# A feature-crossing ranking model on one core: eight fields of the second tile made by products, and a shorter pause ahead of each gather

## What is computed

```python
e = stack([tbl_f[ids[:, f]] for f in range(24)], axis=1)      # 1024 x 24 x 16
def cin(X0, Ws):                                              # three layers of 64
    Xk = X0
    for W in Ws:
        Xk = einsum('bfd,bhd,fho->bod', X0, Xk, W.reshape(24, Xk.shape[1], 64))
        outs.append(Xk.sum(axis=2))
    return concatenate(outs, axis=1)
h = concatenate([cin(e, (W0, W1, W2)), dense_ctx], axis=1)
y = relu(relu(h @ W_top1 + b_top1) @ W_top2 + b_top2) @ W_top3
```

## Time and profile before

| | |
|---|---|
| median of 3 runs | 396.9 us (392.81 to 399.77) |
| the profiled execution: its time | 396.69 us |
| the profiled execution: its span | 394.8 us |
| mean granted TensorE clock | 0.978 of full speed |
| busy: PE, DVE, ACT, POOL | 356.2, 305.0, 185.2, 245.0 us |
| busy share: PE, DVE, ACT, POOL | 90%, 77%, 47%, 62% |
| moved by DMA | 71.07 MB, mean 180 GB/s |

### The profile page before, as it was taken

The page is one execution under the profiler, slowest core; times in us unless marked ns, Lnnn a source line. Parts: engine busy times, 40 slices in busy tenths (PEclk is TensorE's granted clock), DMA queues, the critical chain, the costliest instruction groups (busy, mean ns, idle before and its releaser), DMA issues.

```text
span 394.8 us, 6950 instructions
## 1 busy us (share of the span) xinstructions
PE 356.2 (90%) x2624; PEld 156.3 (40%) x2624; DVE 305.0 (77%) x299; ACT 185.2 (47%) x347; POOL 245.0 (62%) x348
## 2 busy tenths in 40 slices
PE   0866899999919999999999996999999999999997
PEld 0545422423302334444433342434352445343475
DVE  2881399699618899989889967979798979998700
ACT  1120024352032457584647428565656486646464
POOL 5888888888888888888878888888880000000000
PEclk9999899999967999999999999899999999999999
DMA  7557958970999879994999789998998899750000
GB/s 208 166 115 154 235 116 175 229 167 6 202 239 253 204 157 235 255 262 94 225 249 237 146 201 261 248 203 200 250 250 202 186 247 247 210 161 0 2 2 2
DMA packets 56885, 71.07 MB, mean 180 GB/s; under 512 B 31154, under 2 KB 36018, under 8 KB 56851
## 3 DMA queue, kind: packets, MB, share of 16 engines
q1 hardware_dynamic: 49138, 69.04, 73.4%
q0 software_dynamic: 5632, 1.45, 3.6%
q10 hardware_dynamic: 2080, 0.13, 0.4%
HBM read 50.15 MB, written 1.58 MB: 131 GB/s over the span
## 4 chain that ended last, share of the span: by engine, by line
PE 46%; DMA 21%; issue 12%; DVE 11%; SPq 5%; ACT 2%; POOL 2%; ACTq 0%; DVEq 0%; POOLq 0%
PE ps_x L405 28%; DMA B_sb<-x_sb 9%; DVE Z L382 7%; PE ps_tower L405 7%; PE ps_b L405 6%; DMA C<-x_scratch 4%; PE ps_turn L405 4%; DMA A<-x_scratch 3%; DVE Z L345 2%; PE ps_turn L458 2%; SPq L257 2%; DMA small_ids_sb<-small_ids 1%; DMA x_scratch<-x_rows 1%; POOL x_rows L215 1%; DMA x_rows<-tbl,ids_sb 1%
## 5 line engine op out<-in xcount | busy, mean ns | idle before, releaser
L382 DVE TENSOR_TENSOR Z<-A,ps_b 128x1024 f32<-128x1024 f32 x192 | 221.0, 1215 | 8.4 <-PE ps_x L405 4.1
L215 POOL DMA_INDIRECT x_rows<-tbl,ids_sb x176 | 184.6, 1049 | 51.9 <-POOL pause_sb L226 31.7
L405 PE MATMUL ps_x<-Z,w_sb 128*64 128x512 f32 x768 | 185.2, 601 | 0.7 <-DVE Z L382 0.5
L372 DVE TENSOR_TENSOR Z<-A,C 128x1024 f32<-128x1024 f32 x48 | 58.2, 1225 | 49.4 <-DMA A<-x_scratch 24.5
L405 PEld LDWEIGHTS ps_x<-Z,w_sb 128*64 128x64 f32 x768 | 49.4, 137 | 81.0 <-issue 61.3
L405 PE MATMUL ps_x<-Z,w0s_sb 128*64 128x512 f32 x192 | 48.3, 625 | 16.6 <-DVE Z L372 15.0
L226 POOL MEMSET pause_sb<- 128x288 f32 x168 | 60.2, 358 | 0.2
L690 ACT ACTIVATE x_diag<-ps_turn,mask_sb 128x192 f32<-128x192 f32 x128 | 50.6, 606 | 11.9 <-PE ps_turn L466 7.8
L673 ACT COPY ps_b<-B_sb 128x1024 f32<-128x1024 f32 x36 | 36.9, 1026 | 14.2 <-DMA B_sb<-x_sb 13.8
L703 ACT COPY G<-ps_turn 128x416 f32<-128x416 f32 x31 | 15.7, 506 | 52.5 <-PE ps_turn L405 46.9
L405 PEld LDWEIGHTS ps_turn<-x_diag,x_rows 128*64 128x64 f32 x496 | 25.1, 137 | 17.8 <-issue 16.1
(11 more groups left out here) (60 smaller groups left out, 182.7 us busy)
## 6 DMA issues: line engine op xcount, KB each, us to landing
A<-x_scratch SPq DMA_DIRECT2D x48, 512.0 KB
B_sb<-x_sb SPq DMA_DIRECT2D x72, 256.0 KB
C<-x_scratch SPq DMA_DIRECT2D x32, 512.0 KB
x_rows<-tbl,ids_sb POOLq DMA_INDIRECT x176
x_quarters<-x_scratch SPq DMA_DIRECT2D x16, 96.0 KB
x_scratch<-x_rows SPq DMA_DIRECT2D x7, 192.0 KB
small_ids_sb<-small_ids SPq DMA_DIRECT2D x2, 512.0 KB, 5.3
w_sb<-w SPq DMA_DIRECT2D x2, 384.0 KB
```

Of the source, the lines that this page charges most:

```text
L215: pool.indirect_dma_start(out=x0_rows[t % 2][:, f * D:(f + 1) * D], out_offset=None, in_=tables[f], in_offset=bass.IndirectOffsetOnAxis(ap ...
L372: nc.vector.tensor_tensor(Z[s % ZR][:, :], A[u % AS][i][:, :], C[u % 2][i][:, :], ALU.mult).then_inc(z_ready, 1)
L382: nc.vector.tensor_tensor(Z[s % ZR][:, :], A[u % AS][i][:, :], ps_b[j % 2][:, :], ALU.mult)\
L405: return nc.tensor.matmul(out, lhsT, rhs, start=start, stop=stop)
```

## The change

Fields 8 to 15 (set 0) of tile 1 are no longer gathered but made by products with ones, as they are for tile 0. `MADE` lists what is made so, as pairs of tile and set. GpSimd gathers 16 fields of tile 1 and not 24, and its pause writes 144 columns and not 288.

The ids of the third set are read into `small_ids_sb[0]` once the cast of set 0 of tile 0 has read it: SyncE waits for that ahead of this load, and so ahead of the loads of the identity and the first weights. VectorE makes the new ones behind the preparation of the weights and ahead of the first `cross1`. TensorE multiplies them in the same loop, so `turn_small(1)` now stands behind the third chunk of the new set, and `turn_small(2)` behind its last. ScalarE copies the result into `x0_rows[1]`, and `store_tile(1)` waits for it too.

```diff
-PAUSE = 288
+PAUSE = 144
+MADE = ((0, 0), (0, 1), (1, 0))
...
-    HOT = [(k, c) for k in range(SETS) for c in range(chunks[k])]
+    HOT = [(m, c) for m, (t, k) in enumerate(MADE) for c in range(chunks[k])]
...
+        def gathered_fields(t):
+            made = [k for m, k in MADE if m == t]
+            return [f for f in range(F) if f < FR or f // FR - 1 not in made]
+        def gathers(t):
+            return sum(len(gathered_fields(m)) for m in range(1, t + 1))
...
-                for f in range(F):
+                for n, f in enumerate(gathered_fields(t)):
                     pool.memset(pause_sb[:, :], 0.0).then_inc(paused, 1)
-                    pool.wait_ge(paused, F * (t - 1) + f + 1)
+                    pool.wait_ge(paused, gathers(t - 1) + n + 1)
...
+            sp.wait_ge(small_ids_ready, SETS + 1)
+            src = small_ids[SETS:SETS + 1, :].to_broadcast([CR, FR * TILE_ROWS])
+            sp.dma_start(small_ids_sb[0][:, :], src).then_inc(next_ids_in, 16)
             sp.dma_start(id_sb[:, :], ident).then_inc(ident_in, 16)
...
             def store_tile(t):
-                sp.wait_ge(gathered[t % 2], 16 * F * ((t + 1) // 2))
+                if t % 2 == 1:
+                    sp.wait_ge(gathered[1], 16 * (gathers(1) + F * (t // 2)))
+                else:
+                    sp.wait_ge(gathered[0], 16 * F * (t // 2))
+                if t == 1:
+                    sp.wait_ge(small_ready, len(MADE))
...
+            make_ones(0)
+            make_ones(1)
             dve.wait_ge(mask_in, 16)
...
+            make_ones(2)
             for i in range(NI):
                 cross1(0, i)
...
-                if c == 2 and k > 0:
-                    turn_small(0)
-            turn_small(SETS - 1)
+                if c == 2 and m > 0:
+                    turn_small(m - 1)
+            turn_small(len(MADE) - 1)
             keep_warm(WARM[0])
...
-            for k in range(SETS):
-                act.wait_ge(hot_used, sum(chunks[:k + 1]))
+            for m, (t, k) in enumerate(MADE):
+                act.wait_ge(hot_used, made_hot[m])
...
-                act.wait_ge(small_ready, k + 1)
-                store_rows(act, 0, slice(FR * (k + 1), FR * (k + 2)), part_stored[k + 1])
+                if t == 0:
+                    act.wait_ge(small_ready, m + 1)
+                    store_rows(act, 0, slice(FR * (k + 1), FR * (k + 2)), part_stored[k + 1])
```

More of the change, by code:

```diff
@@ L71, in cin_tower @@
     CR = small_tables.shape[0]
-    HOT = [(k, c) for k in range(SETS) for c in range(chunks[k])]
+    SETS_AT = [sum(chunks[:k]) for k in range(SETS)]
+    HOT = [(m, c) for m, (t, k) in enumerate(MADE) for c in range(chunks[k])]
+    made_hot = [sum(chunks[k] for t, k in MADE[:m + 1]) for m in range(len(MADE))]
     x0_dram = nc.dram_tensor("x0_scratch", [TILES, F, 2 * COLS], F32, kind="Internal").ap()
@@ L218, in gather @@
                 ).then_inc(landed, 16)
-            for f in range(FR):
+            for f in gathered_fields(0):
                 gather(0, f, first_gathered)
@@ L338, in _, with make_ones @@
             dve.wait_ge(small_rows_in, 16)
-            for n, (k, c) in enumerate(HOT):
-                if c == 0:
+            def make_ones(m):
+                t, k = MADE[m]
+                if t == 0:
                     dve.wait_ge(small_ids_in[k], 16)
-                    nc.vector.tensor_copy(small_ids_f32[k][:, :], small_ids_sb[k][:, :]).then_inc(small_ids_ready, 1)
-                    dve.wait_ge(small_ids_ready, SETS + k + 1)
-                after(dve, hot_used, n - ZR + 1)
-                nc.vector.tensor_scalar(Z[n % ZR][0:CR, :], small_ids_f32[k][:, :], small_rows_sb[:, c:c + 1],
-                                        None, ALU.is_equal).then_inc(hot_ready, 1)
+                else:
+                    dve.wait_ge(next_ids_in, 16)
+                nc.vector.tensor_copy(small_ids_f32[k][:, :], small_ids_sb[k][:, :]).then_inc(small_ids_ready, 1)
+                dve.wait_ge(small_ids_ready, SETS + m + 1)
+                for c in range(chunks[k]):
+                    n = HOT.index((m, c))
+                    after(dve, hot_used, n - ZR + 1)
+                    nc.vector.tensor_scalar(Z[n % ZR][0:CR, :], small_ids_f32[k][:, :], small_rows_sb[:, c:c + 1],
+                                            None, ALU.is_equal).then_inc(hot_ready, 1)
+            make_ones(0)
+            make_ones(1)
             dve.wait_ge(mask_in, 16)
@@ L906 @@
         "ids": ids.reshape(TILES, 128, F).transpose(1, 0, 2).reshape(128, TILES * F),
-        "small_ids": ids[0:TILE_ROWS, FR:].transpose(1, 0).reshape(SETS, FR * TILE_ROWS),
+        "small_ids": np.concatenate([ids[TILE_ROWS * t:TILE_ROWS * (t + 1), FR * (k + 1):FR * (k + 2)].transpose(1, 0)
+                                     .reshape(1, FR * TILE_ROWS) for t, k in MADE]),
         "small_tables": small_tables.reshape(FR, sum(chunks), cr, D).transpose(2, 1, 0, 3),
```

25 lines of the change are left out of this document (18 added, 7 removed).

## The result

| | before | after |
|---|---|---|
| median of 4 runs each | 395.21 us (392.81 to 399.77) | 377.41 us (375.55 to 380.43) |
| ratio, with its 95% interval | | 0.9576 (0.9471 to 0.9682) |
| the profiled execution: time, span | 396.69, 394.8 us | 375.55, 373.7 us |
| mean granted TensorE clock | 0.978 | 0.991 |

Faster, by 17.8 us between the medians and by 21.1 us between the two profiled executions, where 12.4 were forecast. The profiled execution of after was the fastest of its four, so what follows splits a gain that is somewhat larger than the usual one. Two later measurements of the same kernel gave 376.17 us, ratio 0.9493 (0.9446 to 0.9539), and 377.78 us, ratio 0.9516 (0.9434 to 0.9598).

A forecast was written before the change was run, and what follows sets the result against it. Late gathers starving loads of tile 2, then TensorE, were taken as the bound. 396.7 + 4.0 (opening) - 10.9 (stall) - 5.5 (steady waits) = 384.3 us; range 379 to 392.

The forecast's parts named there:

- The stall at tile 2: Before unit 4, first to read tile 2: earlier gathers let its loads land in time, so the whole 10.9 us goes.
- The opening: Start of the kernel up to the last `cross1(0)`: new products with ones cost 4.0 us, bounds 3 and 5.
- Both chains: In the opening: TensorE's work to the last `cross1(0)`, 3.9 us later; store of fields 16 to 23 delaying C, 1.8 to 4.5.
- The steady part: The 11 units from `turn_x2(2)` to `turn_x2(13)`: of 8 us of waits 5.5 go, bounds 0 and 9.
- Steady waits stay: Rival, units after the stall: DMA and SyncE's order keep the waits, 389.8 us; chance 0.17.
- The port lock: Rival, opening: VectorE's cast and comparisons hold GpSimd for 7.5 us, the stall half returns, 387.5 us; chance 0.06.
- My row-based figure: Opening: judged by a gather of 1.10 us beside comparisons, eight comparisons cost GpSimd under 1 us.
- A dearer opening: Rival: store of fields 16 to 23 or moved weights late by twice the estimate, start slips by 9, 389.3 us; chance 0.05.
- Slower, the pause kept gathers short: Rival, GpSimd: half the pause lengthens gathers, period 1.9 us, every tile bound by GpSimd, 409 us; chance 0.04.

The follow-up runs named there:

- the two halves: Changed kernel with the old pause of 288 columns: 386.04 us; kernel before with only the pause cut to 144 columns: 384.25 us.
- the kernel with the pause alone: The kernel before with its pause cut from 288 to 144 columns and nothing else: 384.25 us, ratio 0.9645.
- six kernels here: Changed kernel without pacing rule (422.1 us), also with five loads in front (416.18), with rule holding nothing (448.84), with pauses of 16 (425.18), 72 (429.23), 216 columns (399.65).

## Why the prediction was wrong

**The stall at tile 2: right.** 10.9 forecast, 11.1 measured. The first gather of tile 2 was to stand at about 40 us and does at 40.22, that of tile 3 at 79 and does at 78.54; the pause was to take 250 ns and takes 252. `store_tile(2)` came at 83.27, not 80: the profile has SyncE wait for the gathers to land, and the last of tile 2 had been issued by 78.04. It cost nothing, as VectorE did not wait. C of unit 4 was issued at 89.71, not 94, since `turn_x0(1)` came at 82.33 and not at 88. The table of the two halves confirms the split: the 8 gathers do it, not the pause.

**The opening: the step that failed.** The forecast was +4.0, ending at 50.5. In the first profile it was -1.3, ending at 45.27, and over all profiles (three after, two before) +0.5, which is no change that they can tell. Both chains of the working started from VectorE's end of the weights, "28.31 + 0.36 = 28.67", as if that were fixed, and added the new work behind it. The weights end at 23.86, 22.84 and 23.48 us in the three profiles of the changed kernel, some 5 us earlier.

Of the 4.8 us in the first profile 2.9 lie ahead of the cast of set 1, where the old profile has its hole, which I read as part of the kernel's course. Both profiles of the kernel before have it, but the kernel with the pause alone, which is the same up to there, does not, so the change did not take it away. It has the crawl's mark (17 and 28 matmuls from 12 to 16 us, 56 and 56 after). The second of the two belongs to a batch with the crawl. For the first no batch is on record, so whether the kernel before would be free of it beside a changed kernel that is free is not shown. Another 1.6 us are the ten comparisons, 8.50 in the old profile and 6.94 beside the shorter pause. They are an effect of the change that I missed. I looked for what the comparisons do to GpSimd and never asked what GpSimd's pauses do to the comparisons, though 0.85 us each in set 1 against 0.69 each in the first three of set 0 stood in the old profile.

What followed from this start came out so. The dummy transposes were to start at 39.2 and start at 33.92, 31.93 and 33.14. The store of fields 16 to 23 was to be issued at 33.5, 4.4 later than before; it was issued at 29.29, 28.02 and 28.48, where the two profiles of before have 29.06 and 29.02. So it did not slip, and gave C no cause to.

It is luck that the stretch from the end of the weights to the end of the opening agrees with my sum in the first profile, 45.27 - 23.86 = 21.4 us against 50.5 - 28.7 = 21.8. There TensorE's own chain ends last, as in the sum. In the other two the stretch takes 24.2 and 23.3, and VectorE waits for C ahead of the last product, as it did before. The second profile of the changed kernel:

```profile
44.70 1.24 DVE L402 TENSOR_TENSOR Z<-A,C 128x1024 f32<-128x1024 f32 x1 [2.80 <-DMA C<-x_scratch]
46.00 1.08 PE L436 MATMUL ps_x<-Z,w0s_sb 128*64 128x512 f32 x4 [1.06 <-DVE Z L402]
```

From the issue of the store to that of C it took 3.8, 7.5 and 6.8 us there, and 5.2 and 3.0 in the two profiles of before. I had put this at half of 5.2 for the changed kernel. Why it varies so was not traced.

**The steady part: right in kind, too small.** I took 5.5 of 8 us of waits with bounds of 0 and 9; 8.7 went, and on average over the five profiles as much. Three profiles of the changed kernel give 212.8, 212.8 and 215.5 us for the 11 units, against my 216. That is the second term that was mis-sized, by 3.2 us. I had held loads to fit "with little room" by the 254 GB/s of one window, but that was a rate seen and not a limit shown: from 7 to 9 us the kernel before moved 416 GB/s. The third profile has one long unit left (21.9 us), which shows what is still scarce:

```profile
262.69 1.20 POOL L230 DMA_INDIRECT x_rows<-tbl,ids_sb  x1 [0.27 <-POOL pause_sb L241]
...
268.51 1.02 ACT L712 COPY ps_b<-B_sb 128x1024 f32<-128x1024 f32 x1 [3.97 <-DMA B_sb<-x_sb]
```

The chances leant on the wrong worry. I held the loads to be the next bound and gave that 0.17; in two of three profiles no unit is longer for them.

**The range.** Its low end, 379, was the forecast with every hidden term at its best, but with the opening never better than +3. A lower one was asked for there. The pause's share in the comparisons measures 1.6 us for the ten of set 1 and 1.1 for the eight new ones (8 x 0.85 against 5.71); taken from +4.0 that leaves +1.3, and with it as the bound the low end is 377.

**The rivals.** *Steady waits stay*: fell, as above. *The port lock*: the place was right and the price between. From the gather at 23.93 to that at 30.63, beside the new cast and ones, three periods take 6.70 us where three alone take 4.35, so GpSimd lost 2.4 us. My row-based figure was under 1, the whole length of cast and ones is 6.4. The Trainium skill, "SBUF — State Buffer", "Who interferes with whom", is borne out in that one engine's instruction holds the other off until it ends: the pause of 0.23 us takes 0.69. That GpSimd stands still for the whole stretch of cast and comparisons was my reading of it, and the trace speaks against that: GpSimd gets in between two comparisons, and with a pause of 288 columns the comparison is the one that takes longer. *A dearer opening*: fell. *Slower, the pause kept gathers short*: fell in its own terms. Gathers average 1068 ns beside 144 columns and 1057 beside 16, before 1049. What goes with the long ones is in the timelines: of the 30 gathers above 1.15 us in the profile of after, 26 run beside a product A x C of VectorE (`cross1`), of the other 138 only 11; before it is 23 of 24, and 20 of the other 152. No run was made to test this.

## What to carry to other kernels

A row from the middle of an opening is not a fixed point. Before work is added behind it, ask whether the change reaches what stands ahead of it, and whether a hole in it is there in a second execution. When one engine writes SBUF in short bursts beside another's elementwise work, price the meeting in both directions; here the one that paid changed between bursts of 144 and of 288 columns. And a slow result deserves a run of the unaltered kernel in the same batch before it is explained: six kernels here were 22 to 71 us slower than the changed one, and the four of them that were run again were not. The same goes for a gain: with one profile of each side the opening seemed to end 1.3 us earlier, and my sum for the new work in it seemed right.

## What the runs showed of the hardware that I had not expected

- The crawl. TensorE issues 4 or 5 matmuls per gather of GpSimd (period 1.4 us with 72 columns) with DMA at a share of 0.03 to 0.08, at 1.2 as at 2.4 GHz. It lasts from 12 to about 38 us in the runs with 72 and with 16 columns, and for 4 to 8 us in the opening of the other four, and it returns in later units as long as GpSimd gathers. Meanwhile VectorE waits up to 10.5 us and ScalarE up to 34.1 us for a `remote` event. In the 16-column run TensorE issued 39 matmuls from 14 to 20 us and, once GpSimd stood still, 118 from 40 to 46. In these runs it came by batch; neither the kernel nor the chip decided it alone. What does was not found.
- In the kernel before it seems to show only as a hole of some 2 us, and its time does not suffer: 397.5 and 397.3 us in the batches with the crawl, 395.2 to 398.2 in the others. That a kernel that waits for its gathers anyway hides it is my reading, and no run shows it.
- A memset on GpSimd and a comparison on VectorE exclude each other for whole instructions: 0.69 us for 0.23, or 1.14 for 0.73.
